# Mixture stage: combine weights and normalized rows are turned by DMA transposes instead of by TensorE

## The reference

```python
xn = rms_norm(x, gamma_x)                      # (512, 256) for each sequence
logits = einsum('bsd,etd->bset', xn, se)       # 512 tokens x 1024 slots
dispatch = softmax(logits, axis=1)             # over tokens
slots = einsum('bsd,bset->betd', xn, dispatch) # 1024 x 256
processed = gelu(slots @ w1) @ w2              # 1024 x 256
combine = softmax(logits.reshape(b, s, e*t))   # over slots
out = einsum('bnd,bsn->bsd', processed, combine)
```

## Time and profile before

| | us |
|---|---|
| median of 3 runs | 2584.41 |
| lowest, highest | 2579.6, 2589.17 |
| span of the profiled execution | 2581.7 |
| PE, DVE, ACT, POOL busy in it | 2337.3, 1892.3, 1681.8, 880.3 |

### The profile page before, as it was taken

One profiled execution on the slowest core, in us unless ns is written; L12 is line 12 of the kernel. 1 busy time (PEld: TensorE's weight loads), 2 busy tenths in 40 slices (PEclk: granted clock), 3 DMA queues, 4 the chain that ended last, 5 costly groups with the idle time before them and its releaser, 6 DMA issues.

```text
span 2581.7 us, 54517 instructions
## 1 busy us (share of the span) xinstructions
PE 2337.3 (91%) x22748; PEld 1779.9 (69%) x22748; DVE 1892.3 (73%) x3201; ACT 1681.8 (65%) x2940; POOL 880.3 (34%) x631
## 2 busy tenths in 40 slices
PE   2889989888999998999898989989898989999999
PEld 2556666666777776777676767667676768777788
DVE  8788889997896887777878777668777774542631
ACT  4476666555757684776757575757767586675666
POOL 1222122212413221363536344453626264132122
PEclk9899999998999998999999999999999999999999
DMA  5000000000000000000000000000000000000000
GB/s 177 19 1 1 1 1 1 1 1 1 1 1 1 1 1 26 2 18 10 14 14 14 14 4 24 2 26 2 14 22 14 22 2 10 9 1 9 9 10 9
DMA packets 34981, 33.08 MB, mean 13 GB/s; under 512 B 7664, under 2 KB 34096, under 8 KB 34736
## 3 DMA queue, kind: packets, MB, share of 16 engines
q1 hardware_dynamic: 34736, 29.60, 3.5%
HBM read 12.54 MB, written 4.19 MB: 6 GB/s over the span
## 4 chain that ended last, share of the span: by engine, by line
PE 67%; DVE 18%; ACT 7%; issue 4%; POOL 2%; SPq 1%; DMA 1%; DVEq 0%; ACTq 0%
PE psum L747 17%; PE psum L749 16%; PE psum L748 16%; PE psum L753 6%; PE psum L1174 2%; PE psum L1176 2%; PE psum L1025 2%; PE psum L1175 2%; PE psum L1078 2%; DVE a1pr L1939 1%; PE psum L1055 1%; ACT a1PT L1481 1%; DVE a1nm L1916 1%; POOL a1pr L2177 1%; SPq L722 1%
## 5 line engine op out<-in xcount | busy, mean ns | idle before, releaser
L2190 POOL TENSOR_TENSOR f1hT<-f1g,f1hT 128x512 f16<-128x512 f32 x256 | 306.6, 1202 | 641.3 <-ACT f1hT L1584 640.5
L2177 POOL TENSOR_TENSOR a1pr<-a1PT,a1pr 128x1024 f16<-128x1024 f32 (+1 forms) x176 | 360.7, 2051 | 293.4 <-DVE a1pr L1939 293.3
L747 PE MATMUL psum<-f1sl,f1w1h 128*128 128x256 f16 x1024 | 285.1, 278 | 9.8 <-ACT f1g L1579 7.7
L747 PE MATMUL psum<-f1w2h,f1hT 128*128 128x256 f16 x1024 | 281.4, 275 | 6.1 <-issue 3.9
L748 PE MATMUL psum<-f1sl,f1w1h 128*128 128x256 f16 x1024 | 284.6, 278 | 0.0
L749 PE MATMUL psum<-f1sl,f1w1l 128*128 128x256 f16 x1024 | 284.3, 278 | 0.0
L748 PE MATMUL psum<-f1w2l,f1hT 128*128 128x256 f16 x1024 | 280.5, 274 | 0.0
L749 PE MATMUL psum<-f1w2h,f1hT 128*128 128x256 f16 x1024 | 280.4, 274 | 0.0
L1916 DVE TENSOR_REDUCE a1nm<-psum 128x2 f32<-128x768 f32 (+3 forms) x176 | 197.9, 1124 | 59.5 <-PE psum L1005 58.4
L1939 DVE CAST a1pr<-a1PT 128x1024 f16<-128x1024 f32 (+1 forms) x176 | 173.6, 988 | 77.6 <-ACT a1PT L1481 64.0
L2166 POOL TENSOR_TENSOR f0h<-f0Y,f0sc 128x704 f32<-128x704 f32 x64 | 91.4, 1428 | 326.4 <-DVE f0Y L1786 326.3
(11 more groups left out here) (344 smaller groups left out, 6904.1 us busy)
## 6 DMA issues: line engine op xcount, KB each, us to landing
a1Q<-a1st SPq DMA_DIRECT2D x96, 64.0 KB, 2.6
a1K<-a1st SPq DMA_DIRECT2D x96, 64.0 KB, 2.6
x<-in_L_attn_x SPq DMA_DIRECT2D x8, 512.0 KB, 8.0
out<-x SPq DMA_DIRECT2D x8, 512.0 KB, 3.0
wslot<-in_L_ffn_w SPq DMA_DIRECT2D x1, 1024.0 KB, 8.7
wraw<-in_L_ffn_w SPq DMA_DIRECT2D x1, 1024.0 KB, 5.9
wslot<-in_L_ffn_slot_embeds SPq DMA_DIRECT2D x1, 1024.0 KB, 8.2
a1Q<-a1mr SPq DMA_DIRECT2D x64, 4.0 KB, 1.7
```

What stands on the lines that cost most here:

```text
L747: e.matmul(out, lh, rh, start=start, stop=False)
L2177: e.tensor_tensor(a1["pr"][:, i % 2, 1, :, 0:w], a1["PT"][:, i % 2, :, 0:w], a1["pr"][:, i % 2, 0, :, 0:w], ALU.subtract).then_inc(s["a1_pl"])
L2190: e.tensor_tensor(hT1[:, c % 2, 1, 2 * hp:2 * hp + 2, :], gg[:, hp % 2, :, :], hT1[:, c % 2, 0, 2 * hp:2 * hp + 2, :], ALU.subtract).then_ ...
```

## The change

Both turns of the stage leave TensorE. For the logits, the halves `xn_h` and `xn_l`, which exist anyway, are turned by eight DMA transposes (128x256 fp16 each), issued by SyncE. For the combine weights, ScalarE and VectorE split the exponentials in SBUF, into `ub`, a view that lies on `xn`'s storage and has one place for each half hf, and two DMA transposes (128x512 fp16) for each of the eight pieces write `eT`. The third pair of PSUM banks in `f1_banks` goes away. The rehearsal gets a cost for a DMA transpose, which is that of a copy of the same bytes.

```diff
+    def dma_start_transpose(self, out, src):
+        return self.note(60, None, 2.0 * out.shape[0] * self.each(out))
...
@@ SyncE
+            def f1_rows(j):
+                S = at_f1(j)
+                for t in range(NT):
+                    yield S + 10.0 + 0.3 * t
+                    q.wait_ge("f1_nh", j + 1)
+                    q.wait_ge("f1_nl", j + 1)
+                    q.wait_ge("f1_lg", 8 * j)
+                    for m, rows in enumerate((xn_h, xn_l)):
+                        e.dma_start_transpose(f1xT[:, m, :, qrows(t)], rows[:, t, 0:D]).then_inc(s[f"f1_x{t}"], 16)
+
+            def f1_second(j):
+                S = at_f1(j)
+                for n in range(8):
+                    t, hf = divmod(n, 2)
+                    yield S + f1_e2_at(n) + 2.4
+                    q.wait_ge("f1_ul", 8 * j + n + 1)
+                    q.wait_ge("f1_cb", 2 * j)
+                    for m in range(2):
+                        e.dma_start_transpose(eT[:, m, 4 * hf:4 * hf + 4, qrows(t)], ub[:, hf, m, :]).then_inc(s[f"f1_t{hf}"], 16)
...
@@ TensorE
             def f1_front(j):
-                    for t in range(NT):
-                        ins = tr(v[:, t * P:(t + 1) * P], xn[:, t, k * P:(k + 1) * P])
-                    ins.then_inc(s["f1_xT"])
...
+                    q.wait_ge(f"f1_x{t}", 32 * (j + 1))
...
-            def f1_second(j):                                 # TensorE
...
-                    for i in range(4):
-                        ins = tr(v[:, i * P:(i + 1) * P], u[:, n % 2, i * P:(i + 1) * P])
-                    ins.then_inc(s["f1_eT"])
...
@@ TensorE
             def f1_combine(j):
-                                q.wait_ge("f1_Tl", 8 * j + 4 * tp + 4)
+                                q.wait_ge("f1_t0", 32 * (4 * j + 2 * tp + 2))
+                                q.wait_ge("f1_t1", 32 * (4 * j + 2 * tp + 2))
...
@@ ScalarE
             def f1_front(j):
-                    e.activation(f1xT[:, 0, k, :], psum[:, 4 + k, :], ACT.Copy).then_inc(s["f1_xh"])
...
@@ ScalarE
             def f1_second(j):
-                    q.wait_ge("f1_eT", 8 * j + n - 1)
+                    q.wait_ge("f1_ul", 8 * j + n - 1)
...
-                    e.activation(eT[:, 0, 4 * hf:4 * hf + 4, qrows(t)], psum[:, f1_banks(j)[2][n % 2], :].rearrange("p (i s) -> p i s", i=4),
-                                 ACT.Copy).then_inc(s["f1_Th"])
+                    q.wait_ge("f1_ex", 8 * j + n + 1)
+                    q.wait_ge("f1_nl", j + 1)
+                    q.wait_ge(f"f1_t{hf}", 32 * (4 * j + t))
+                    e.activation(ub[:, hf, 0, :], u[:, hf, :], ACT.Copy).then_inc(s["f1_uh"])
...
@@ VectorE
             def f1_front(j):
+                q.wait_ge("f1_t0", 128 * j)
+                q.wait_ge("f1_t1", 128 * j)
...
-                    e.tensor_tensor(f1xT[:, 1, k, :], psum[:, 4 + k, :], f1xT[:, 0, k, :], ALU.subtract).then_inc(s["f1_xl"])
...
@@ VectorE
             def f1_second(j):
-                    e.tensor_tensor(eT[:, 1, js, qrows(t)], psum[:, f1_banks(j)[2][n % 2], :].rearrange("p (i s) -> p i s", i=4), eT[:, 0, js, qrows(t)],
-                                    ALU.subtract).then_inc(s["f1_Tl"])
+                    e.tensor_tensor(ub[:, hf, 1, :], u[:, hf, :], ub[:, hf, 0, :], ALU.subtract).then_inc(s["f1_ul"])
```

More of the change, by code:

```diff
@@ L100, in f1_banks @@
 def f1_banks(j):
-    return ((4, 5), (4, 5), (4, 5)) if j < B + LATE else ((4, 5), (0, 1), (2, 3))
+    return ((4, 5), (4, 5)) if j < B + LATE else ((4, 5), (0, 1))
 A0_GROUPS = (((0,), 4, P), ((1,), 5, P), ((3, 2), 6, 0))
@@ L601, in build @@
         xn = sb("f1xn", [P, NT, D], f32, stD)
+        ub = xn[:, :, :].rearrange("p t d -> p (t d)").bitcast(f16).rearrange("p (i m n) -> p i m n", i=2, m=2)
         dd = sb("f1d", [P, NS], f32, stD)
@@ L735, in last @@
                 q.wait_ge("out", 16 * B)
-            return [weights(), *[chain(z, B) for z in (load, a1_moves, store)], last()]
+            return [weights(), *[chain(z, B) for z in (load, a1_moves, store)],
+                    *[chain(z, 2 * B) for z in (f1_rows, f1_second)], last()]
         def tensor(e, q, banks):
@@ L1106, in f1_front @@
                 S = at_f1(j)
[L1107 to L1111, removed]
-                    for t in range(NT):
-                        ins = tr(v[:, t * P:(t + 1) * P], xn[:, t, k * P:(k + 1) * P])
-                    ins.then_inc(s["f1_xT"])
-                    banks.after(bk, "f1_xl", 2 * j + k + 1)
                 for n in range(8):
                     t, hf = divmod(n, 2)
-                    yield S + 10.0 + 2.3 * n
+                    yield S + 12.5 + 2.0 * n
                     q.wait_ge("w_l", W_L["se", 3])
@@ L1187, in f1_slots2 @@
                     banks.after(f1_banks(j)[1][1], "f1_sx", n + 1)
-            def f1_second(j):
[L1190 to L1196, removed]
-                    for i in range(4):
-                        ins = tr(v[:, i * P:(i + 1) * P], u[:, n % 2, i * P:(i + 1) * P])
-                    ins.then_inc(s["f1_eT"])
-                    banks.after(bk, "f1_Tl", 8 * j + n + 1)
             def f1_mlp(j):
@@ L1262, in tensor @@
                   *[chain(z, B) for z in (a0_front, a0_values, a0_scores, a0_mix, a0_out, a1_front, a1_first, a1_maxima, a1_second, a1_values, a1_out)],
-                  *[chain(z, 2 * B) for z in (f1_front, f1_slots, f1_slots2, f1_second, f1_mlp, f1_mlp2, f1_combine)]]
+                  *[chain(z, 2 * B) for z in (f1_front, f1_slots, f1_slots2, f1_mlp, f1_mlp2, f1_combine)]]
         def scalar(e, q, banks):
@@ L1500, in f1_front @@
                 S = at_f1(j)
-                for k in range(2):
-                    yield S + 7.3 + 1.0 * k
-                    q.wait_ge("f1_xT", 2 * j + k + 1)
-                    e.activation(f1xT[:, 0, k, :], psum[:, 4 + k, :], ACT.Copy).then_inc(s["f1_xh"])
                 for n in range(8):
                     t, hf = divmod(n, 2)
-                    yield S + 11.5 + 2.3 * n
+                    yield S + 13.8 + 2.0 * n
                     q.wait_ge("f1_lg", 8 * j + n + 1)
@@ L1518, in f1_rows @@
             def f1_rows(j):
-                yield at_f1(j) + 9.5
+                yield at_f1(j) + 6.5
                 q.wait_ge("f1_u", 4 * j + 4)
@@ L2001, in f1_front @@
                     e.tensor_scalar(xn[:, t, :], xb[:, b, t, :], mv[:, t, 0:1], rstd[:, 2, t:t + 1], ALU.subtract, ALU.mult).then_inc(s["f1_u"])
-                for k in range(2):
-                    yield S + 8.0 + 1.0 * k
-                    q.wait_ge("f1_xh", 2 * j + k + 1)
-                    e.tensor_tensor(f1xT[:, 1, k, :], psum[:, 4 + k, :], f1xT[:, 0, k, :], ALU.subtract).then_inc(s["f1_xl"])
                 for t in range(NT):
@@ L2034, in f1_rows @@
             def f1_rows(j):
-                yield at_f1(j) + 10.5
+                yield at_f1(j) + 7.6
                 q.wait_ge("f1_nh", j + 1)
@@ L2075, in f1_second @@
                     t, hf = divmod(n, 2)
-                    yield S + f1_e2_at(n) + 3.1
-                    q.wait_ge("f1_Th", 8 * j + n + 1)
-                    js = slice(4 * hf, 4 * hf + 4)
-                    e.tensor_tensor(eT[:, 1, js, qrows(t)], psum[:, f1_banks(j)[2][n % 2], :].rearrange("p (i s) -> p i s", i=4), eT[:, 0, js, qrows(t)],
-                                    ALU.subtract).then_inc(s["f1_Tl"])
+                    yield S + f1_e2_at(n) + 1.6
+                    q.wait_ge("f1_uh", 8 * j + n + 1)
+                    e.tensor_tensor(ub[:, hf, 1, :], u[:, hf, :], ub[:, hf, 0, :], ALU.subtract).then_inc(s["f1_ul"])
                 yield S + 72.0
```

6 lines of the change are left out of this document (1 added, 5 removed), and 4 rows, old and new, of the table s.

## The result

The change made the kernel slower: 2668.36 us median (2667.62 to 2671.26, 4 runs) against 2582.4 us in the same session, a ratio of 1.0331 with a 95% interval of 1.0316 to 1.0345. The span of the profiled execution is 2666.5 us, 84.8 us more than before.

The account below looks back on a forecast made before the run. The prediction took TensorE as the bound: -59 us for removed transposes, +76 combine-weight loop, +30 front, +25 a1 moves, sum +72 on a span of 2581.7 us, some 2655 us median. Range 2540 to 2900 us.

Parts of the forecast that it names:

- the likeliest case: Whole kernel: T from 2.3 to 4.5 us, time 2594 to 2784 us, likeliest 2655; chance 0.37.
- T: SyncE's queue: time one 128x512 fp16 DMA transpose holds it, taken as 3.1 us, the middle of 1.5 to 6.2.
- The lower bound: SyncE's queue: if transposes move in pieces like plain copies, issue decides and T = 0.6 us.
- One of 128x256 takes T/2: Front's transposes on SyncE's queue: half the bytes hold the queue for half of T.
- The formula: Whole kernel, change in us: -59 + 5.6(4T - 4.1) + 12.6(4T - 10, if positive) + 17.7T.
- The steady round: Combine-weight loop: two halves need four transposes, 4T = 12.4 us, against gaps of 4.1 us (j = 12 to 15) or 10.
- The long first gaps and j = 0 to 2 are covered: Combine-weight loop: no ScalarE stops counted at each stage's long first gap or in stages 0 to 2.
- The 70% that TensorE feels: Combine-weight loop: TensorE loses 70% of ScalarE's stops, (66 + 43) x 0.7 = +76 us.
- the 59 us: TensorE: gain from 640 transposes removed, 85% of 70 us, -59 us.
- both hidden: 0: Combine weights: SBUF casts (+4 us, ScalarE) and subtractions (+12 us, VectorE) add nothing to the span.
- my fast rival: Whole kernel: T under 1 us, as copies are; sum -42, 2542 us; chance 0.25.
- My rival above T = 4.5: SyncE's queue is the bound, not TensorE; at T = 6.2, +353 us, 2937 us; chance 0.23.

Follow-up runs that it names:

- merged kernel: Against the changed kernel, order frozen: high and low half of a combine-weight piece turned by one 128x1024 DMA transpose instead of two 128x512; 2594.15 us.
- the cut one: Against the changed kernel, order frozen: each 128x512 DMA transpose issued as two of 128x256, same bytes; 2898.17 us.
- the pair with one place and two: Against the changed kernel, order frozen: only the high half turned, output not the reference's; one place per half 2585.58 us, two places 2564.30 us.
- the two best of the frozen and new orders: Against the changed kernel: high half only with two places, frozen, 2564.30 us; 128x1024 combine-weight transposes, rehearsal told 1270 ns, order anew, 2576.19 us.
- the kernel with the merged front: Against the changed kernel: combine weights and the front's low rows in 128x1024 transposes, rehearsal told 1270 ns, order anew; 2597.18 us.

## Why the prediction was right, and where it was wrong

The time, 2668 us for a forecast of 2655, fell in the likeliest case. The path was the right one: `ub`'s one place, ScalarE behind SyncE's queue, TensorE behind ScalarE. The price under it was wrong, and that the total still came out is luck.

**T.** The step that failed is "I take T = 3.1 us". It was 1.27 us, and it is not made of bytes: the same for 64, 128 and 256 KB. The transposes went out in packets of 238 bytes in the mean (176128 packets more for 41.99 MB), between the 32-byte pieces that I assumed and the 852 bytes of the copies. The merged kernel has 4096 packets fewer with 128 instructions fewer, the cut one 8192 more with 256 more: 32 go with each instruction. The other 163840 carry the data, by that count 256 bytes each, one row of 128 fp16 values. The lower bound was the nearer one: an issue time like the 0.594 us row, and not the gathering, sets T. "One of 128x256 takes T/2" failed too. The formula with T = 1.27 us alone gives -59 + 5.5 + 22.5 = -31, so some 2553 us, on the wrong side. With the fixed 1.25 us for the smaller ones as well, the formula's terms become -59, +6 (5.6 x (4 x 1.27 - 4.1)), +24 for the front (10 us for 12.4) and +20 for a1 (10 for 12): -9 on the span. Measured was +85. So the sum holds an error of 94 us the other way, and the forecast was right in its size because two errors cancelled.

**Where the 94 us are.** The steady round explains only part of the stops. With T = 1.27 us it leaves stops in the eight close rounds alone, 8 us in all. The forecast put 66 us into j = 12 to 15 and 43 us into j = 3 to 11. Summed from ScalarE's timeline the waits are 28.2 us in j = 12 to 15 (from 2212 us on) and 76.8 us in j = 3 to 11 (960 to 2212 us), where at 5.2 us a round and gaps of 10 us there should have been none. The largest part that the forecast lacked is in "The long first gaps and j = 0 to 2 are covered": 47.2 of the 113.8 us are waits of the third and fourth cast of a stage, right behind that gap, because the transposes before them are held by s_f1_cb until the last stage's combine ends, and a long gap doesn't help. Next, the transposes stand behind the a1 moves in the one queue (8.6 us of issue for twelve; 23.4 us in three waits, one of which is among the 47.2). The a1 moves were seen as something that the transposes delay; that they delay the transposes was not in the sum. That the transposes also hold the storage for the next stage's `xn` (VectorE's 30.0 us) had no term. To that comes an order built with 60 ns for each transpose, up to 46 us, and the lower clock, below. How the 94 us divide among these is not shown.

**The total of ScalarE's waits.** Forecast 109 us, measured 113.8, but not "over 5 us each": 66 waits of 1.7 us in the mean, three over 7. The 70% that TensorE feels can't be read from the change itself. In the pair with one place and two it was 21 of 41 us, half.

**The front and the a1 moves.** Alone, the front cost 23 us net. Its own share of the 59 us is a fifth, 12, so the turned rows' lateness would be 35 us, for 30 forecast; but 23 us is hardly more than two freshly built orders lie apart, and beside merged transposes the front cost nothing, so the agreement is not shown to be more than chance. TensorE waited for them only 11.4 us in the change. The moves of a1 cost TensorE 17.3 us of waits for 11.5 before: +6 in place of +25. The combine weights alone cost 68 us, and with their four fifths of the 59 us given back, 115 for the 76 forecast.

**The work.** ScalarE's casts took 629 ns, as read from the like row. VectorE's subtractions in SBUF took 903 ns in the mean, for 0.78 forecast; the median is 692, and the rest is a tail up to 2.5 us that the PSUM form before did not have (max 693 ns). The row by form:

```profile
L2075 DVE TENSOR_TENSOR f1xn<-f1u,f1xn 128x512 f16<-128x512 f32 x128 | 115.2, 903 | 79.6 <-ACT f1xn L1567 79.5
```

It lies in the loop of the place, on the path from cast to transpose, so "both hidden: 0" was not safe. What it cost wasn't tried by itself.

**TensorE's 70 us.** They went: the two best of the frozen and new orders are busy 2274.4 and 2274.1 us, 63 less than before. In the change it was 36.5 us. The same 22108 matmuls took 2274 us at a clock of 0.957 and 0.962, 2289.1 at 0.947, 2300.8 at 0.943 and 2334.9 at 0.908, so busy time grows as the clock falls; not strictly, since the kernel with the merged front has 2294.5 at 0.952. So the span's +85 is -70 for the transposes, +121 of idle time, and +33 of busy time, which is what is left and goes with the lower clock. The forecast had no term for the 33 us. No run held the clock apart from the idle time, so that the one brings the other is read from these rows, not shown.

**The figures of the Trainium skill.** The Trainium skill's page "VectorE: DVE Perf Modes", section "The three transpose paths", from which I had worked out 5.2 us for four blocks, does not hold here as a price of a block: four blocks land 2.4 us after the start of issue, and eight in the merged kernel after 2.7, with the queue held 1.23 to 1.27 us. The advice of the same page of the Trainium skill, section "Rules for kernel authors", to use TensorE for a 128x128 transpose where PSUM will do as its destination, fits the result for this change. The Trainium skill's page "DMA: Bandwidth & Descriptors", section "Latency and other measured facts", gives 261 GB/s for DMA transposes. The engines' added time agrees roughly: 11.0% of 2666.5 less 3.5% of 2581.7 us is 203 us for 41.99 MB, 207 GB/s, an engine time of 0.6 us for 128 KB. But that was not the bound, and my fast rival, which took T to be small when bytes are fast, missed the time to issue.

**Rivals.** That bytes or the DMA engines bind is refuted by the merged and cut kernels. My rival above T = 4.5, that the queue is the bound, is what the cut kernel came nearest to: 2898 us, with SyncE at 20% of the chain and TensorE still at 52%.

## What to carry to other kernels

Price a DMA transpose by the instruction, not the byte, and put as many blocks as the layout allows into one: here halving the count of the larger ones turned +3.3% into +0.4%. A buffer that is freed by a DMA ties its writer to everything that stands ahead in that queue, so look at what it is queued behind and at what that waits for, and give it a second place, before counting a round of the loop. Freshly built orders of nearly the same work lay up to 0.8% apart, so freeze the order where an effect is smaller than that.

## What the runs showed of the hardware

SyncE's issue of a DMA transpose takes 1.23 to 1.27 us, whether it is 128x256, 128x512 or 128x1024 fp16, twice that of a plain move (0.594 us), and landing comes 2.4 us after the start of issue (2.7 us for 128x1024). The DMA engines move it in packets of some 240 bytes in the mean and need about half the issue time for 128 KB. A VectorE subtraction of 128x512 with both operands in SBUF took 692 ns in the median like the form with one in PSUM (682), but up to 2.5 us at times; whom it met there was not tried.
